# One-hots built 12 blocks at a time in two buffers, in a graph message-passing kernel

## The chip, the cores and the metric

The kernel runs on one core of a Trainium2 chip. The metric is the device time of one execution in microseconds (us), where lower is better. A core has TensorE (PE, with its weight loads as PEld), VectorE (DVE), ScalarE (ACT), GpSimd (POOL) and SyncE (SP), which run their own instruction streams in order and wait for each other on semaphores.

## The reference

A graph with 3125 nodes and 53125 sorted edges passes two layers of messages. Each message is linear, so the sum over the edges of a node needs only the sum of the neighbours' rows, the number of edges and the sum of their attributes.

```python
def _mp_layer(x, src, dst, edge_attr, W, b):
    n = x.shape[0]
    loops = jnp.arange(n, dtype=src.dtype)
    src2 = jnp.concatenate([src, loops])
    dst2 = jnp.concatenate([dst, loops])
    ea2 = jnp.concatenate([edge_attr, jnp.zeros((n, edge_attr.shape[1]), dtype=edge_attr.dtype)], axis=0)
    msg = jnp.concatenate([x[dst2], x[src2], ea2], axis=1) @ W + b
    return jax.nn.relu(jax.ops.segment_sum(msg, dst2, num_segments=n))
...
h = jax.nn.relu(_mp_layer(x, src, dst, edge_attr, W1, b1))
out = jax.nn.log_softmax(_mp_layer(h, src, dst, edge_attr, W2, b2), axis=1)
return _layernorm(x + out, axis=-1)
```

## The kernel before

The 3125 nodes are 25 tiles of 125 nodes. The kernel makes the adjacency matrix in bf16 once, in a tensor `adj`, and then multiplies it with the node rows of layer 1 (x, written as three bf16 parts in `x3`) and of layer 2 (`z3`, three parts too).

**Edges to keys.** The edges fall into 625 blocks (in the code: windows) of at most 128 edges; block w holds the edges into five consecutive target nodes. GpSimd gathers the edges in five groups of 125 blocks (`gather_edges(j)`, `gather_attrs(j)`). VectorE turns each edge into two numbers, seven operations per group (`key_distances`, `key_tiles`, `key_sums`). TensorE turns them around (`turn_keys`) and ScalarE copies them to `keys` (`copy_keys`), one column per block.

**Keys to the matrix.** VectorE makes two one-hot tensors from each column of keys: `ohl` and `ohr`, 125 columns each (`onehots`). TensorE multiplies the two, one matmul per block, into PSUM (`build(k)`: set k is the blocks 8k to 8k+7). ScalarE copies each set from `pset` to `adj` (`evacuate(k)`). There are 79 sets. The one-hots of a set lie in one of three buffers, so `onehots(k)` waits until set k-3 is built: `dve.wait_ge(built, k - 2)`.

**Layer 1.** The matmuls with x3 use the same block numbers: group g of 25 blocks is the target tile g. TensorE's order is written by hand:

```python
for b in range(NSETS):
    if b + LEAD < NSETS:
        build(b + LEAD)
    ...
        layer1(g, h, h + n)
```

LEAD is 4. So one set is built (8 matmuls), then eight matmuls of layer 1 that stand four sets behind, and so on. After each three groups there is an epilogue i, spread over three successive sets b by `turn_block(i)`: `turn_sums`, `hidden`, `messages`. VectorE does its smaller work after the one-hots of particular sets k: the group sums `reduce_sums(g)` at `last_set_block(g) + 6`, `z_rest(i)` and `z_low(i)` of the epilogues, the keys of the next group, the attribute sums and once the bias weights (at k = 10).

**Layer 2** starts when the last set has been used: 625 matmuls (`layer2`), with VectorE's final softmax and normalisation in six batches behind it.

**The start.** SyncE loads the first 12 tiles of x, the weights and the bias rows, and loads the other 13 tiles of x once the first edges have come. ScalarE casts x to its first part (`cast_x`), VectorE subtracts that (`x_rest`), ScalarE casts the middle part, VectorE makes the low part; the first `layer1` waits for all of it. GpSimd splits the bias rows into three bf16 parts (`blink`) after all ten gathers.

Of the kernel before, what the change touches and what calls it, by code (L numbers as in the profile page):

```python
# [68 lines left out]
ROUND = 12582912.0  # L69
MID = N // 2  # L70
# [3 lines left out]
def gnn(nc, x, x_tiles, dst, edges, edge_attr, W1, b1, W2, b2, out, E):  # L74
# [3 lines left out]
    with ExitStack() as ctx:  # L78
        def sb(name, shape, dt):
            return ctx.enter_context(nc.sbuf_tensor(name, shape, dt))  # L80
# [53 lines left out]
        hi_q = tail([Q, J, SLOTS], FP32)  # L134
        lo_f = tail([Q, J, SLOTS], FP32)
        hi_f = tail([Q, J, SLOTS], FP32)
        w_f = tail([Q, J, SLOTS], FP32)
        p_f = tail([Q, J, SLOTS], FP32)
# [23 lines left out]
        ohl = [sb(f"ohl{s}", [128, SET // 2, Q, 2], BF16) for s in range(3)]  # L162
        ohr = [sb(f"ohr{s}", [128, SET // 2, G * WD, 2], BF16) for s in range(3)]
# [124 lines left out]
        xs_ready = sem("xs_ready")  # L288
        bchain = sem("bias_chain")
# [33 lines left out]
        def _(gp):  # L323
# [18 lines left out]
            gp.iota(iota2[:, :, :], [[1, SLOTS], [0, 2]], base=0, channel_multiplier=0,  # L342
# [18 lines left out]
            gather_edges(0)  # L361
            gather_attrs(0)
# [24 lines left out]

            p0, p1, p2 = (bpart[:, k, :] for k in range(3))
            r0, r1 = brest[:, 0, :], brest[:, 1, :]
            done = [1]  # L390

            def blink(ins):
                done[0] += 1
                ins.then_inc(bchain, 1)
                gp.wait_ge(bchain, done[0])

            gp.wait_ge(bchain, 1)
            gp.wait_ge(b_in, 16 * 4)
            blink(gp.tensor_copy(p0, brows))
            blink(gp.tensor_tensor(r0, brows, p0, ALU.subtract))  # L400
            blink(gp.tensor_copy(p1, r0))
            blink(gp.tensor_tensor(r1, r0, p1, ALU.subtract))
            gp.tensor_copy(p2, r1).then_inc(bchain, 1)
# [35 lines left out]
        def _(dve):  # L439
# [51 lines left out]
            def key_distances(j):  # L491

                dve.wait_ge(pairs_in[j], 16)
                dve.wait_ge(loops_ready, 2)
                ins = dve.tensor_scalar(d_f[:, j, :], pairs[:, j, 1::2], thr[:, j:j + 1], None, ALU.subtract)
                dve.tensor_scalar(hi_q[:, j, :], pairs[:, j, 0::2], 1.0 / Q, 0.5 / Q - 0.5, ALU.mult, ALU.add)
                link(ins)

            def key_tiles(j):

                link(dve.scalar_tensor_tensor(out=w_f[:, j, :], in0=d_f[:, j, :], scalar=-float(WD - 1),
                                              in1=d_f[:, j, :], op0=ALU.add, op1=ALU.mult))
                link(dve.tensor_scalar(hi_f[:, j, :], hi_q[:, j, :], ROUND, ROUND, ALU.add, ALU.subtract))

            def key_sums(j):

                dve.tensor_scalar(p_f[:, j, :], w_f[:, j, :], 0.0, 8192.0, ALU.is_gt, ALU.mult)
                link(dve.scalar_tensor_tensor(out=m_f[:, j, :], in0=hi_f[:, j, :], scalar=float(WD),
                                              in1=d_f[:, j, :], op0=ALU.mult, op1=ALU.add))
                dve.scalar_tensor_tensor(out=lo_f[:, j, :], in0=hi_f[:, j, :], scalar=-float(Q), in1=pairs[:, j, 0::2],  # L510
                                         op0=ALU.mult, op1=ALU.add)
                dve.tensor_tensor(key_f[:, j, :], m_f[:, j, :], p_f[:, j, :], ALU.add).then_inc(key_ready, 1)
# [9 lines left out]
            def onehots(k):  # L522

                n = -(-set_size(k) // 2)
                if k >= 3:
                    dve.wait_ge(built, k - 2)
                for oh, key in ((ohl, keyl), (ohr, keyr)):
                    ins = dve.tensor_tensor(  # L528
                        out=oh[k % 3][:, 0:n, :, :],
                        in0=iota2[:, 0:Q, :].unsqueeze(1).broadcast_to([128, n, Q, 2]),  # L530
                        in1=key[:, k * SET:k * SET + 2 * n].rearrange("p (q o k) -> p q o k", o=1, k=2)
                        .broadcast_to([128, n, Q, 2]),
                        op=ALU.is_equal)
                ins.then_inc(oh_ready, 1)

# [28 lines left out]
            key_distances(0)  # L564
            key_tiles(0)
            key_sums(0)
            dve.wait_ge(consts, 8)
            dve.wait_ge(keys_ready, 1)
            for k in range(3):
                onehots(k)  # L570
            dve.wait_ge(xs_ready, 2)
            dve.tensor_tensor(x_rest, x_nat[:, :, :], x3[:, :, 0:C], ALU.subtract).then_inc(xs_rest, 1)
            onehots(3)
            dve.wait_ge(xs_ready, 3)
            dve.tensor_tensor(x3[:, :, 2 * XC:2 * XC + C], x_rest, x3[:, :, XC:XC + C], ALU.subtract).then_inc(xs_ready, 1)
            attr_sums(0, 0, WD)

            for k in range(4, NSETS):
                for j in range(1, J):
                    if k * SET <= j * Q < (k + 1) * SET:  # L580
                        dve.wait_ge(keys_ready, j + 1)
                onehots(k)
# [167 lines left out]
        def _(act):  # L750
# [11 lines left out]

            cast_x(0, 0, XA)

            def copy_keys(bank, j):
                act.wait_ge(keyt_done, j + 1)
                act.activation(keys[:, :, j * Q:(j + 1) * Q], bank.rearrange("p (t w) -> p t w", t=2), ACT.Copy)\  # L767
                   .then_inc(keys_ready, 1)

            copy_keys(acc[0][:, 0:2 * Q], 0)  # L770
            cast_x(1, XA, G)
# [52 lines left out]
            for k in range(3):  # L824
                evacuate(k)
            act.wait_ge(xs_rest, 1)
            act.activation(x3[:, :, XC:XC + C], x_rest, ACT.Copy).then_inc(xs_ready, 1)
            evacuate(3)
# [66 lines left out]
        def _(pe):  # L895
# [245 lines left out]
```

## Time and profile before

| | |
|---|---|
| time, median of 3 runs | 218.02 us (217.85 to 218.08) |
| profiled execution, its own time | 218.17 us |
| profiled execution, its span | 216.4 us |
| PE busy | 181.1 us (84%) |
| DVE busy | 175.5 us (81%) |
| ACT busy | 118.6 us (55%) |
| POOL busy | 43.0 us (20%) |

The span is the part of an execution that the profile's rows cover. Busy time is the sum over an engine's instructions, where overlap counts once. A wait is told as idle time of the waiting instruction's engine, with the instruction that ended it.

### The profile page before, as it was taken

How to read it: one execution, taken by the hardware profiler on the slowest of the kernel's cores; microseconds unless marked ns; L12 is line 12 of the kernel's file. 1: busy time of each engine (PE TensorE's matmuls, PEld its weight loads, DVE VectorE, ACT ScalarE, POOL GpSimd, SP SyncE). 2: the span in 40 equal slices, each digit the busy share in tenths (PEclk: the TensorE clock that was granted, in tenths of full speed). 3: DMA queues.
4: the chain of work that ended last, by engine and by line, in shares of the span. 5: the costliest groups of instructions: out<-in, count | busy, mean ns of one | idle time of the engine just before them, and what ended most of it. 6: DMA issues, size and time to landing. Idle time of an engine off the chain costs nothing.

```text
span 216.4 us, 5159 instructions
## 1 busy us (share of the span) xinstructions
PE 181.1 (84%) x2044; PEld 164.2 (76%) x2044; DVE 175.5 (81%) x510; ACT 118.6 (55%) x225; POOL 43.0 (20%) x61
## 2 busy tenths in 40 slices
PE   0516278799989999999899999999999999999920
PEld 0105178687978998888779979989899999999910
DVE  1879799999899999999998999962025956999881
ACT  2415537569878897887887988976221201011110
POOL 7478873002200395004003000000000000000000
PEclk9999999999999999999999999999999999999995
DMA  1433010000000000000000000000000010101000
GB/s 39 104 101 109 23 13 3 0 3 1 5 2 3 2 3 0 3 0 3 0 3 0 5 0 3 2 3 0 3 0 3 0 39 0 23 17 27 18 18 21
DMA packets 8649, 3.25 MB, mean 15 GB/s; under 512 B 7910, under 2 KB 8175, under 8 KB 8625
## 3 DMA queue, kind: packets, MB, share of 16 engines
q1 hardware_dynamic: 7825, 1.98, 4.4%
q0 software_dynamic: 800, 0.93, 1.8%
q8 instruction: 17, 0.28, 0.5%
q14 instruction: 7, 0.06, 0.1%
HBM read 2.09 MB, written 0.81 MB: 13 GB/s over the span
## 4 chain that ended last, share of the span: by engine, by line
PE 60%; DVE 24%; DMA 7%; ACT 3%; issue 3%; ACTq 0%; DVEq 0%
PE pset L975 17%; PE acc L932 15%; PE pset L918 12%; PE acc L975 8%; DVE ohr L528 7%; DVE ohl L528 6%; DMA x_nat<-in_x_tiles 3%; PE epb L959 3%; DMA adj<-in_edges,adj 2%; DMA adj<-in_dst 2%; PE epb L947 2%; PE epb L967 2%; DVE adj L518 1%; ACT adj L784 1%; PE epb L960 1%
## 5 line engine op out<-in xcount | busy, mean ns | idle before, releaser
L784 ACT ACTIVATE adj<-pset 125x1000 bf16<-125x1000 f32 (+7 forms) x100 | 81.1, 837 | 19.2 <-PE pset L918 15.2
L932 PE MATMUL acc<-x,adj 125*125 125x195 bf16 x625 | 67.1, 250 | 0.0
L918 PE MATMUL pset<-ohr,ohl 128*125 128x125 bf16 x625 | 54.7, 232 | 13.8 <-DVE ohr L528 11.5
L918 PEld LDWEIGHTS pset<-ohr,ohl 128*125 128x125 bf16 x625 | 46.9, 145 | 20.0 <-issue 9.3
L932 PEld LDWEIGHTS acc<-x,adj 125*125 125x125 bf16 x625 | 56.4, 138 | 0.3
L528 DVE TENSOR_TENSOR ohl<-iota,keys 128x1000 bf16<-128x1000 bf16 (+1 forms) x79 | 53.1, 672 | 1.4 <-ACT keys L767 1.3
L528 DVE TENSOR_TENSOR ohr<-iota,keys 128x1000 bf16<-128x1000 bf16 (+1 forms) x79 | 52.9, 669 | 0.0
L975 PE MATMUL pset<-z,adj 125*125 125x192 bf16 x425 | 36.9, 247 | 0.0
L975 PEld LDWEIGHTS pset<-z,adj 125*125 125x125 bf16 x425 | 35.5, 136 | 0.4 <-issue 0.2
L860 ACT ACTIVATE x<-x 125x192 f32<-125x192 f32 (+2 forms) x6 | 2.6, 426 | 31.7 <-DVE x L651 31.7
L377 POOL CAST stats<-se 125x15 bf16<-125x15 f32 x5 | 5.8, 1164 | 66.1 <-DMA se<-se_scratch 66.1
L975 PE MATMUL acc<-z,adj 125*125 125x192 bf16 x200 | 17.6, 247 | 0.0
L975 PEld LDWEIGHTS acc<-z,adj 125*125 125x125 bf16 x200 | 16.8, 136 | 0.1
L542 DVE TENSOR_REDUCE u<-acc 125x65 f32<-125x195 f32 x25 | 8.8, 354 | 6.1 <-PE acc L932 6.0
L550 DVE TENSOR_TENSOR u<-epb,z 125x192 f32<-125x192 f32 (+1 forms) x9 | 3.1, 340 | 11.5 <-ACT z L817 11.5
L358 POOL DMA_INDIRECT adj<-in_edge_attr,adj x5 | 9.2, 1833 | 1.5 <-issue 1.5
L901 PE MATMUL pset<-adj 125*125 125x426 f16 x4 | 2.2, 608 | 7.3 <-DVE adj L459 7.3
L354 POOL DMA_INDIRECT adj<-in_edges,adj x5 | 6.8, 1368 | 4.2 <-DVE adj L476 3.0
L816 ACT ACTIVATE base<-epb 125x192 f32<-125x192 f32 (+1 forms) x9 | 2.9, 319 | 8.7 <-PE epb L969 8.7
L901 PEld LDWEIGHTS pset<-adj 125*125 125x125 f16 x4 | 0.7, 180 | 8.3 <-DVE adj L449 6.1
L641 DVE TENSOR_REDUCE x<-pset 125x64 f32<-125x192 f32 x17 | 5.5, 351 | 1.8 <-PE pset L975 1.7
L799 ACT ACTIVATE u<-x_nat,u 125x64 f32<-125x64 f32 x25 | 6.8, 338 | 0.0
(123 smaller groups left out, 180.0 us busy)
## 6 DMA issues: line engine op xcount, KB each, us to landing
x_nat<-in_x_tiles SPq DMA_DIRECT2D x1, 406.2 KB
x_nat<-in_x_tiles SPq DMA_DIRECT2D x1, 375.0 KB
out<-x SPq DMA_DIRECT2D x2, 187.5 KB
out<-x SPq DMA_DIRECT2D x3, 93.8 KB
adj<-in_dst SPq DMA_DIRECT2D x1, 208.5 KB
out<-x SPq DMA_DIRECT2D x1, 125.0 KB
adj<-in_edges,adj POOLq DMA_INDIRECT x5, 4.4
adj<-in_edge_attr,adj POOLq DMA_INDIRECT x5, 4.5
```

Source lines behind the costliest of these rows:

```text
L354: gp.indirect_dma_start(pairs[:, j, 0:2 * (SLOTS - LOOPS)], None, edges, bass.IndirectOffsetOnAxis(off_idx[:, j:j + 1], 0)).then_inc(pairs ...
L358: gp.indirect_dma_start(attrs[:, j, 0:SLOTS - LOOPS], None, edge_attr, bass.IndirectOffsetOnAxis(off_idx[:, j:j + 1], 0)).then_inc(attrs_i ...
L377: gp.tensor_copy(s0, v.unsqueeze(2).broadcast_to(wide)).then_inc(sech, 1)
L528: ins = dve.tensor_tensor(out=oh[k % 3][:, 0:n, :, :], in0=iota2[:, 0:Q, :].unsqueeze(1).broadcast_to([128, n, Q, 2]), in1=key[:, k * SET: ...
L542: dve.tensor_reduce(u[i % 2][:, m, C:2 * C + 1], acc[g % 2][0:Q, 0:XW].rearrange("p (t c) -> p c t", t=3), AX.X, ALU.add)\
L641: dve.tensor_reduce(f_o[:, g - a, :], bank2(g)[0:Q, :].rearrange("p (t c) -> p c t", t=3), AX.X, ALU.add).then_inc(acc2_read, 1)
L784: ins = act.activation(adj4[0:Q, g, :, i * WD:(i + n) * WD].rearrange("p h (w e) -> p h w e", e=WD), rows[:, w - k * SET:w - k * SET + n, ...
L799: ins = act.activation(u[i % 2][:, m, 0:C], x_nat[:, a + m, :], ACT.Copy, scale=u[i % 2][:, m, 2 * C:2 * C + 1])
L918: ins = pe.matmul(pset[k % 2][0:Q, i // 4, i % 4 * 128:i % 4 * 128 + WD * G], ohl[k % 3][:, i // 2, :, i % 2], ohr[k % 3][:, i // 2, :, i ...
L932: ins = pe.matmul(acc[g % 2][0:Q, 0:XW], adj4[0:Q, g, h, :], x3[:, h, :], start=(h == 0), stop=(h == G - 1))
L959: pe.matmul(epb[:, 0, 0:n], w1c[:, :], flat(i)[:, 0:n], start=True, stop=False)
L975: ins = pe.matmul(bank2(g)[0:Q, :], adj4[0:Q, g, h, :], z3[:, h, :], start=(h == 0), stop=(h == G - 1))
```

## The change

Four edits are made together.

1. The one-hots are no longer made per set of 8 blocks in three buffers. They are made per chunk: the first chunk has 8 blocks, the second 6, then 12 each (14, 26, 38, ...), in two buffers of 12 blocks. Chunk c waits until the set is built that holds the last block of chunk c-2. A set waits for the chunk of its last block. VectorE's smaller work of set k comes after the chunk that holds the set's first block (`beside`).
2. A group's keys take six VectorE operations instead of seven, and two ScalarE copies instead of one.
3. The rest and the low part of x are made in two halves (12 and 13 tiles) at other places of the VectorE and ScalarE streams.
4. GpSimd splits the biases between `gather_edges(0)` and `gather_attrs(0)`.

```diff
+CHUNK = 12
+CHUNKS = ((0, 8), (8, 14)) + tuple((a, min(a + CHUNK, WINDOWS)) for a in range(14, WINDOWS, CHUNK))
+
+
+def chunk_of(w):
+    return next(c for c, (a, b) in enumerate(CHUNKS) if a <= w < b)
...
-        ohl = [sb(f"ohl{s}", [128, SET // 2, Q, 2], BF16) for s in range(3)]
-        ohr = [sb(f"ohr{s}", [128, SET // 2, G * WD, 2], BF16) for s in range(3)]
+        ohl = [sb(f"ohl{s}", [128, CHUNK // 2, Q, 2], BF16) for s in range(2)]
+        ohr = [sb(f"ohr{s}", [128, CHUNK // 2, G * WD, 2], BF16) for s in range(2)]
...
-                ins = dve.tensor_scalar(d_f[:, j, :], pairs[:, j, 1::2], thr[:, j:j + 1], None, ALU.subtract)
-                dve.tensor_scalar(hi_q[:, j, :], pairs[:, j, 0::2], 1.0 / Q, 0.5 / Q - 0.5, ALU.mult, ALU.add)
-                link(ins)
+                dve.tensor_scalar(d_f[:, j, :], pairs[:, j, 1::2], thr[:, j:j + 1], None, ALU.subtract)
+                link(dve.tensor_scalar(q_f[:, j, :], pairs[:, j, 0::2], -float(Q // 2), 1.0 / Q, ALU.add, ALU.mult))
...
-            def onehots(k):
-
-                n = -(-set_size(k) // 2)
-                if k >= 3:
-                    dve.wait_ge(built, k - 2)
+            def onehots(c):
+
+                a, b = CHUNKS[c]
+                n = (b - a + 1) // 2
+                if c >= 2:
+                    dve.wait_ge(built, (CHUNKS[c - 2][1] - 1) // SET + 1)
                 for oh, key in ((ohl, keyl), (ohr, keyr)):
                     ins = dve.tensor_tensor(
-                        out=oh[k % 3][:, 0:n, :, :],
+                        out=oh[c % 2][:, 0:n, :, :],
...
+            key_distances(0)
+            key_tiles(0)
+            key_sums(0)
+            rest_of_x(0, 0, XA)
+            dve.wait_ge(consts, 8)
+            dve.wait_ge(keys_ready, 1)
+            onehots(0)
+            onehots(1)
+            low_of_x(0, 0, XA)
+            onehots(2)
+            rest_of_x(1, XA, G)
+            attr_sums(0, 0, WD)
+            onehots(3)
+            low_of_x(1, XA, G)
+
+            done_sets = 0
+            for c in range(4, len(CHUNKS)):
+                for j in range(1, J):
+                    if CHUNKS[c][0] <= j * Q < CHUNKS[c][1]:
+                        dve.wait_ge(keys_ready, j + 1)
+                onehots(c)
+                sets = range(done_sets, (CHUNKS[c][1] - 1) // SET + 1)
+                done_sets = sets.stop
+                for k in sets:
+                    beside(k)
...
-                pe.wait_ge(oh_ready, k + 1)
+                pe.wait_ge(oh_ready, chunk_of(k * SET + set_size(k) - 1) + 1)
                 for i in range(set_size(k)):
+                    w = k * SET + i
+                    c = chunk_of(w)
+                    q, t = divmod(w - CHUNKS[c][0], 2)
                     ins = pe.matmul(pset[k % 2][0:Q, i // 4, i % 4 * 128:i % 4 * 128 + WD * G],
-                                    ohl[k % 3][:, i // 2, :, i % 2], ohr[k % 3][:, i // 2, :, i % 2], start=True, stop=True)
+                                    ohl[c % 2][:, q, :, t], ohr[c % 2][:, q, :, t], start=True, stop=True)
```

The instruction order of VectorE at the start, from the keys of the first group to the one-hots that the first layer-1 matmuls need (`adj` stands for the scratch tensors that lie in its tail). Before:

```order
L528 TENSOR_TENSOR ohl2<-iota2,keys 128x1000
L528 TENSOR_TENSOR ohr2<-iota2,keys 128x1000
L572 TENSOR_TENSOR adj<-x_nat,x3 125x1600 [waits xs_ready]
L528 TENSOR_TENSOR ohl0<-iota2,keys 128x1000 [waits built]
L528 TENSOR_TENSOR ohr0<-iota2,keys 128x1000
L575 TENSOR_TENSOR x3<-adj,x3 125x25x64 [waits xs_ready]
L518 SCALAR_TENSOR_TENSOR adj<-adj 125x128 [waits attrs_in0]
L518 SCALAR_TENSOR_TENSOR adj<-adj 125x128 x4
L528 TENSOR_TENSOR ohl1<-iota2,keys 128x1000 [waits built]
```

and after the change:

```order
L547 TENSOR_TENSOR adj<-x_nat,x3 125x768 [waits xs_ready]
L536 TENSOR_TENSOR ohl0<-iota2,keys 128x1000 [waits keys_ready,consts]
L536 TENSOR_TENSOR ohr0<-iota2,keys 128x1000
L536 TENSOR_TENSOR ohl1<-iota2,keys 128x750
L536 TENSOR_TENSOR ohr1<-iota2,keys 128x750
L552 TENSOR_TENSOR x3<-adj,x3 125x12x64 [waits xm_ready]
L536 TENSOR_TENSOR ohl0<-iota2,keys 128x1500 [waits built]
L536 TENSOR_TENSOR ohr0<-iota2,keys 128x1500
L547 TENSOR_TENSOR adj<-x_nat,x3 125x832 [waits xs_ready]
```

One subtraction over 25 tiles (`x_rest`) has become one over 12 ahead of the first one-hots and one over 13 behind the third chunk; the low part is split likewise.

VectorE in the long middle stretch, before:

```order
L528 TENSOR_TENSOR ohr1<-iota2,keys 128x1000
L518 SCALAR_TENSOR_TENSOR adj<-adj 125x128 [waits attrs_in2]
L528 TENSOR_TENSOR ohl2<-iota2,keys 128x1000 [waits built]
L528 TENSOR_TENSOR ohr2<-iota2,keys 128x1000
L518 SCALAR_TENSOR_TENSOR adj<-adj 125x128 [waits attrs_in2]
L528 TENSOR_TENSOR ohl0<-iota2,keys 128x1000 [waits built]
```

and after:

```order
L536 TENSOR_TENSOR ohr1<-iota2,keys 128x1500
L561 TENSOR_REDUCE u0<-acc0 125x65 [waits acc_done]
L536 TENSOR_TENSOR ohl0<-iota2,keys 128x1500 [waits built]
L536 TENSOR_TENSOR ohr0<-iota2,keys 128x1500
L580 TENSOR_TENSOR z3<-u1,z3 125x3x64 [waits mid_ready]
L536 TENSOR_TENSOR ohl1<-iota2,keys 128x1500 [waits built]
```

Each pair of one-hot operations still begins with a wait for `built`, but it covers 1500 elements in place of 1000, and the buffers alternate between two.

TensorE, sets 4 to 6 and the layer-1 matmuls between them, before:

```order
L918 MATMUL pset0<-ohr1,ohl1 125x125 [waits oh_ready,evac]
L918 MATMUL pset0<-ohr1,ohl1 125x125 x7
L932 MATMUL acc0<-x3,adj 125x195 [waits keys_ready,xs_ready,evac]
L932 MATMUL acc0<-x3,adj 125x195 x7
L918 MATMUL pset1<-ohr2,ohl2 125x125 [waits oh_ready,evac]
L918 MATMUL pset1<-ohr2,ohl2 125x125 x7
L932 MATMUL acc0<-x3,adj 125x195 x8
L918 MATMUL pset0<-ohr0,ohl0 125x125 [waits oh_ready,evac]
L918 MATMUL pset0<-ohr0,ohl0 125x125 x7
```

and after:

```order
L956 MATMUL pset0<-ohr1,ohl1 125x125 [waits oh_ready,evac]
L956 MATMUL pset0<-ohr1,ohl1 125x125 x5
L956 MATMUL pset0<-ohr0,ohl0 125x125 x2
L970 MATMUL acc0<-x3,adj 125x195 [waits keys_ready,xl_ready,evac]
L970 MATMUL acc0<-x3,adj 125x195 x7
L956 MATMUL pset1<-ohr0,ohl0 125x125 [waits oh_ready,evac]
L956 MATMUL pset1<-ohr0,ohl0 125x125 x7
L970 MATMUL acc0<-x3,adj 125x195 x8
L956 MATMUL pset0<-ohr0,ohl0 125x125 [waits oh_ready,evac]
L956 MATMUL pset0<-ohr0,ohl0 125x125
L956 MATMUL pset0<-ohr1,ohl1 125x125 x6
```

The order of the sets has not moved. Sets 4 and 6 now read from both buffers: 6 blocks from one and 2 from the other, then 2 and 6, while set 5 lies in one buffer.

## Rows read from the trace of the kernel before

**Rows 1.** The page: busy time by engine, and TensorE's granted clock in 40 slices.

```profile
span 216.4 us, 5159 instructions
PE 181.1 (84%) x2044; PEld 164.2 (76%) x2044; DVE 175.5 (81%) x510; ACT 118.6 (55%) x225; POOL 43.0 (20%) x61
...
PEclk9999999999999999999999999999999999999995
```

**Rows 2.** The page: the chain that ended last, shares by line.

```profile
PE pset L975 17%; PE acc L932 15%; PE pset L918 12%; PE acc L975 8%; DVE ohr L528 7%; DVE ohl L528 6%; DMA x_nat<-in_x_tiles 3%; PE epb L959 3%; DMA adj<-in_edges,adj 2%; DMA adj<-in_dst 2%; PE epb L947 2%; PE epb L967 2%; DVE adj L518 1%; ACT adj L784 1%; PE epb L960 1%
```

**Rows 3.** The list of waits: total us, times, longest us.

```profile
PE pset L918 <- DVE ohr L528: 11.5, 11, 4.7
```

**Rows 4.** Timeline of DVE, one-hots; columns are start us, us, instruction.

```profile
39.22 0.66 DVE L528 TENSOR_TENSOR ohl<-iota,keys 128x1000 bf16<-128x1000 bf16 x1
39.81 0.66 DVE L528 TENSOR_TENSOR ohr<-iota,keys 128x1000 bf16<-128x1000 bf16 x1
...
144.19 0.28 DVE L528 TENSOR_TENSOR ohl<-iota,keys 128x250 bf16<-128x250 bf16 x1
```

**Rows 5.** Timeline of PE: a set that waited, and two that did not.

```profile
40.61 0.67 PE L918 MATMUL pset<-ohr,ohl 128*125 128x125 bf16 x8 [0.93 <-DVE ohr L528]
41.12 0.85 PE L932 MATMUL acc<-x,adj 125*125 125x195 bf16 x8
...
132.35 0.64 PE L918 MATMUL pset<-ohr,ohl 128*125 128x125 bf16 x8
...
133.52 0.65 PE L918 MATMUL pset<-ohr,ohl 128*125 128x125 bf16 x8
```

**Rows 6.** Timeline: a group sum on DVE, which waited for PE.

```profile
116.68 0.85 PE L932 MATMUL acc<-x,adj 125*125 125x195 bf16 x8
...
116.96 0.36 DVE L542 TENSOR_REDUCE u<-acc 125x65 f32<-125x195 f32 x1 [0.62 <-PE acc L932]
```

**Rows 7.** Timeline of PE: sets around one epilogue, and set 76.

```profile
94.28 0.67 PE L918 MATMUL pset<-ohr,ohl 128*125 128x125 bf16 x8
...
96.21 0.70 PE L918 MATMUL pset<-ohr,ohl 128*125 128x125 bf16 x8
...
98.44 0.70 PE L918 MATMUL pset<-ohr,ohl 128*125 128x125 bf16 x8
...
100.73 0.70 PE L918 MATMUL pset<-ohr,ohl 128*125 128x125 bf16 x8
...
144.85 0.70 PE L918 MATMUL pset<-ohr,ohl 128*125 128x125 bf16 x8
```

**Rows 8.** Timeline of DVE: the biases' first operation, an epilogue's rest, the next one-hots.

```profile
38.10 0.30 DVE L587 TENSOR_SCALAR adj<-adj,bmask 12x192 f32<-12x192 bf16 x1
...
56.49 0.36 DVE L550 TENSOR_TENSOR u<-epb,z 125x192 f32<-125x192 f32 x1
...
57.34 0.67 DVE L528 TENSOR_TENSOR ohl<-iota,keys 128x1000 bf16<-128x1000 bf16 x1
```

**Rows 9.** Timeline of the start: DVE, then PE (sets 4 and 6).

```profile
12.58 0.29 DVE L495 TENSOR_SCALAR adj<-adj,thr 125x128 f32<-125x128 int32 x1
...
15.77 0.68 DVE L528 TENSOR_TENSOR ohl<-iota,keys 128x1000 bf16<-128x1000 bf16 x1 [1.32 <-ACT keys L767]
...
23.89 1.83 DVE L575 TENSOR_TENSOR x<-adj,x 125x1600 bf16<-125x1600 f32 x1 [1.57 <-ACT x L827]
...
28.03 0.99 DVE L528 TENSOR_TENSOR ohl<-iota,keys 128x1000 bf16<-128x1000 bf16 x1
...
28.25 1.08 PE L918 MATMUL pset<-ohr,ohl 128*125 128x125 bf16 x8 [4.69 <-DVE ohr L528]
...
31.92 0.64 PE L918 MATMUL pset<-ohr,ohl 128*125 128x125 bf16 x8
```

**Rows 10.** Timeline of POOL: first and last of five operations that split the biases.

```profile
26.81 0.76 POOL L399 CAST adj<-adj 12x192 bf16<-12x192 f32 x1
...
30.20 0.67 POOL L403 CAST adj<-adj 12x192 bf16<-12x192 f32 x1
```

More of the change, by code:

```diff
@@ L69 @@
 ROUND = 12582912.0
+LIFT = 64.0
+CODE = 128.0
 MID = N // 2
@@ L288, in gnn @@
         xs_ready = sem("xs_ready")
+        xm_ready = sem("xm_ready")
+        xl_ready = sem("xl_ready")
         bchain = sem("bias_chain")
@@ L361, in _, with blink @@
             gather_edges(0)
+            p0, p1, p2 = (bpart[:, k, :] for k in range(3))
+            r0, r1 = brest[:, 0, :], brest[:, 1, :]
+            done = [1]
+            def blink(ins):
+                done[0] += 1
+                ins.then_inc(bchain, 1)
+                gp.wait_ge(bchain, done[0])
+            gp.wait_ge(bchain, 1)
+            gp.wait_ge(b_in, 16 * 4)
+            blink(gp.tensor_copy(p0, brows))
+            blink(gp.tensor_tensor(r0, brows, p0, ALU.subtract))
+            blink(gp.tensor_copy(p1, r0))
+            blink(gp.tensor_tensor(r1, r0, p1, ALU.subtract))
+            gp.tensor_copy(p2, r1).then_inc(bchain, 1)
             gather_attrs(0)
@@ L385, in split_sums @@
                 gp.tensor_copy(s2, r[:, :, 1:2].broadcast_to(wide)).then_inc(se_parts, 1)
[L388 to L403, printed above, removed]
             for j in range(J):
@@ L562, in z_low, with beside @@
                    .then_inc(z3_ready, 1)
[L564 to L582, printed above, removed]
+            def beside(k):
                 if k == 10:
@@ L761, in cast_x, with cast_middle_x @@
                 act.activation(x3[:, a:b, 0:C], x_nat[:, a:b, :], ACT.Copy).then_inc(xs_ready, 1)
+            def cast_middle_x(i, a, b):
+                act.wait_ge(xs_rest, i + 1)
+                act.activation(x3[:, a:b, XC:XC + C], x_rest[:, a:b, :], ACT.Copy).then_inc(xm_ready, 1)
             cast_x(0, 0, XA)
@@ L766, in copy_keys @@
                 act.wait_ge(keyt_done, j + 1)
-                act.activation(keys[:, :, j * Q:(j + 1) * Q], bank.rearrange("p (t w) -> p t w", t=2), ACT.Copy)\
-                   .then_inc(keys_ready, 1)
+                act.activation(keyl[:, j * Q:(j + 1) * Q], bank[:, 0:Q], ACT.Copy, scale=float(Q),
+                               bias=float(Q // 2) + Q * LIFT + CODE)
+                act.activation(keyr[:, j * Q:(j + 1) * Q], bank[:, Q:2 * Q], ACT.Copy, scale=float(WD),
+                               bias=CODE - WD * LIFT).then_inc(keys_ready, 1)
             copy_keys(acc[0][:, 0:2 * Q], 0)
-            cast_x(1, XA, G)
+            cast_middle_x(0, 0, XA)
             def evacuate(k):
@@ L822, in cast_middle @@
                 act.activation(z3[:, a:b, C:2 * C], u[i % 2][:, 0:b - a, 0:C], ACT.Copy).then_inc(mid_ready, 1)
-            for k in range(3):
+            evacuate(0)
+            cast_x(1, XA, G)
+            evacuate(1)
+            cast_middle_x(1, XA, G)
+            for k in range(2, LEAD):
                 evacuate(k)
-            act.wait_ge(xs_rest, 1)
-            act.activation(x3[:, :, XC:XC + C], x_rest, ACT.Copy).then_inc(xs_ready, 1)
-            evacuate(3)
             for b in range(NSETS):
```

32 lines of the change are left out of this document (17 added, 15 removed).

## The prediction

> **What bounds the kernel now.** I read the page first: PE is busy 84% of the span and DVE 81% [rows 1], so either could bound it. The chain of work that ended last tells more: most of it is matmuls, but 13% is the two one-hot operations of L528 [rows 2]. The list of waits says the same from the other side: PE's sets waited 11.5 us for one-hots in 11 places [rows 3]. Then I read the timelines of both engines from the first set to the last. Where PE does not wait, a set with its eight layer-1 matmuls takes 1.17 us (132.35 to 133.52) [rows 5]; a pair of one-hot operations takes 2 x 0.59 = 1.18 us (start to start 39.22 to 39.81) [rows 4], plus DVE's smaller work. So the two run neck and neck, and three buffers keep them loosely coupled. From set 4 (28.25) [rows 9] to set 76 (144.85) [rows 7] the kernel takes 116.60 us for 72 sets, 1.62 us a set. Behind that comes layer 2, which the change does not touch.
>
> **Part 1: the chunks.** What they promise is fewer DVE instructions: 53 pairs instead of 79. An operation over 1000 elements took 0.66 us, one over 250 took 0.28 [rows 4]: 0.38 us for 750 elements, 0.51 for 1000. The fixed part of the 0.59 us step is thus 0.08 us, and 52 operations fewer save about 4 us of DVE time. An operation over 1500 elements steps 0.59 + 0.25 = 0.85 us and lasts about 0.93.
>
> What they cost is in the wait. The chunks end at blocks 14, 26, 38, 50, ..., and 14 + 12m is never a multiple of 8. Chunk c may begin when the set is built that holds the last block of chunk c-2. That set always holds blocks of chunk c-1 too (the order of PE shows it: 6 blocks from one buffer, 2 from the other), and it can't be built before chunk c-1 is whole. So chunk c can't begin before chunk c-1 has been made, and has been used by a whole set. Two buffers are there, but DVE and PE take turns. One turn, from the start of such a straddling set:
>
> - the set's last matmul ends 0.67 us after its first began [rows 5], and DVE starts about 0.02 later;
> - DVE makes the pair: 0.85 + 0.93 = 1.78 us;
> - PE starts 0.14 us after DVE's end: 39.81 + 0.66 = 40.47 to 40.61 [rows 4, 5].
>
> The sum is 2.61, with rounding 2.62 us for 12 blocks, or 1.75 us a set, where PE needs 1.17. From set 4 (first of chunk 4) to set 76 (first of chunk 52) there are 48 turns: 48 x 2.62 = 125.8 us, as a floor. Three things make single turns longer. I went through all 48, with VectorE's and TensorE's work of each turn from the order:
>
> - *PE's epilogues.* Turns hold one set and two sets in alternation. With an epilogue's parts the distance between sets is 1.93, 2.23 and 2.29 us instead of 1.17 [rows 7]. In a one-set turn this fits into 2.62. In a two-set turn it does not: three turns hold hidden and messages (4.51 us each), two hold sums and hidden (4.18 each, the sums' part lying in the first set) and one the messages alone (3.45). Together 3 x 1.89 + 2 x 1.56 + 0.83 = 9.6 us more.
> - *Group sums.* `reduce_sums(g)` stands behind the chunk that holds the first block of set k. For g = 0 to 7 that set is the second one after the straddling set, and DVE must wait in its place for layer-1 matmuls that PE runs only after the straddling set. The group ends after n matmuls of a piece: n = 2 ended 0.28 us after the piece's start [rows 6], and a matmul more is 0.09. The next chunk begins 0.20 + 0.09 n late. For g = 1 to 6 (n = 2 to 7), with what stands behind the sum in two of them, this is about 4.1 us.
> - *DVE's other work.* Slack for it is 0.69 + 0.14 + 0.07 = 0.9 us a turn. z_rest takes 0.85 (56.49 to 57.34), the bias weights 1.12 (38.10 to 39.22) [rows 4, 8], a group's last key operations some 0.7. Alone they fit or nearly; in eight turns they come together or with the first and last of the eight sums. I count 3.6 us.
>
> So set 4 to set 76 takes 125.8 + 9.6 + 4.1 + 3.6 = 143.1 us at PE's warm pace. One more term: set 4 took 1.08 us where later ones take 0.64 to 0.67 [rows 5, 9], and set 6 started 3.67 us after set 4 rather than 2.34. PE itself bounds that turn, 3.67 instead of 2.62: 1.05 us. Sum 144.2 us against 116.6: **27.6 us more**.
>
> **Part 2: keys.** One dependent operation of about 0.25 us goes from each group. Only the first group's lies on the path: DVE works on it from 12.58, and the one-hots start at 15.77 [rows 9]. ACT's two copies instead of one take about 0.14 us more (a second fixed part, estimated). The later groups' saving is inside the 3.6 above.
>
> **Part 3: x in halves.** Before, DVE stood 1.57 us waiting for ACT's middle part (ahead of 23.89), and 1.32 us for the keys (ahead of 15.77) [rows 9]. The first half's rest, about 0.84 us (1.83 for 25 tiles [rows 9], so 12/25 of it), now fills the second of these, and the 1.57 us are filled by chunks. Against it, set 4 needs 50 blocks instead of 40 (10 blocks x 2 x 0.064 = 1.3 us), and chunk 4 waits some 0.3 us for set 3.
>
> **Part 4: biases.** GpSimd's five operations last 4.06 us (26.81 to 30.87) [rows 10]. In that time a one-hot operation took 0.99 us in place of 0.66 [rows 4, 9]: DVE slows beside them. They now lie beside the first keys. I take 0.4 us of slowing for the key operations, which eats what part 2 gains; bounds are 0 and the whole 4.1 us. By the Trainium skill, page "SBUF — State Buffer", section "SBUF: two separate sides", GpSimd and VectorE hold their shared port pair as an exclusive lock for a whole instruction; by that rule the six key operations could each wait for a GpSimd operation of 0.7 to 0.8 us, so some 2 us or more instead of 0.4. The row on the one-hots shows only 0.33 for one, so I keep 0.4. The gathers behind move about 4 to 6 us later; the attribute sums of group 0 stand after 21 us now, and nothing else needs them soon.
>
> Parts 2 to 4 on the start of set 4: -1.57 - 0.84 + 1.3 + 0.3 + 0.14 - 0.25 + 0.4 = -0.5, I take **-0.6 us** (the slowed one-hot at 28.03 goes too).
>
> **The sum.** 218.17 (the profiled execution; 0.15 above the median) + 27.6 - 0.6 = 245.2; at the end some of VectorE's waits for the last epilogues have been served already, -0.3; on the scale of the median 244.7 us.
>
> **The rivals.**
>
> *A. The turns do not arise* (faster). If DVE can run a chunk ahead after all, PE and DVE overlap as before, and the 4 us of DVE time count where DVE was on the chain, about half, with 0.6 from the start: 218.0 - 2 - 0.6 = 215.4 us. It decides at the mean turn: 116.6/48 = 2.43 us; below that the change wins. For it: both engines need less than that alone (1.76 and 1.70 us per 12 blocks). Against: the waits of the order are not a matter of durations. Chance 6%.
>
> *B. PE's pace falls* (much slower). PE is busy only 1.76 of 2.62 us in a turn. The profile gives the granted clock as 9 throughout [rows 1], yet sets took 1.08 us at 28.25 and 0.64 at 31.92 [rows 9], a half-speed (1.2 GHz) and a full-speed (2.4 GHz) pace. PE had been mostly idle before the slow ones. If it fell back, a turn is 0.41 us longer by the set's end, and a two-set turn about 4.3 us: per pair of turns 7.4 instead of 5.24, so up to 52 us over 24 pairs; half the time, 271 us. Against: a pause of 0.93 us ahead of 40.61 left that set at 0.67 [rows 5]; mine would be up to 1.5. By the Trainium skill, page "TensorE: Matmul & The Clock Gate", section "HAM oscillation — how this bites in real kernels", it is long waits between bursts of matmuls that bring the low clock back; short pauses would then change nothing. Chance 6%.
>
> *C. Turns, but cheaper or dearer pieces.* The same mechanism with a turn off by 0.1 us moves the sum by 4.8; the epilogues' 9.6 us could partly be hidden (minus 5) and the keys' slowing be 2 us more. This is the width of my own case: 237 to 252.
>
> **How the numbers follow.** My case with its width has 88%, rivals A and B 6% each. The range 237 to 254 leaves out both tails. Changes under 0.2% (0.4 us) can't be told from none here. Faster 0.06, same 0.02, slower 0.92.
>
> **What would show it.** After: L536 about 0.93 us for 1500 elements; starts of the pairs about 2.62 us apart in quiet stretches, each right behind the end of a set; waits of PE on one-hots and of DVE on `pset` matmuls in nearly every turn, tens of us in all; the first layer-1 piece half a microsecond earlier; layer 2 as long as before, but beginning some 27 us later. I would be wrong if DVE's pairs follow each other without waits, or if PE's sets of 8 matmuls last over 1 us.

## The result and the profile after

| | before | after |
|---|---|---|
| time, median | 217.94 us (217.72 to 218.08, 4 runs) | 251.34 us (247.00 to 251.66, 4 runs) |
| profiled execution, its own time | 218.17 us | 247.00 us |
| profiled execution, its span | 216.4 us | 245.2 us |

Its executions differ by the granted clock of TensorE: one with a mean of 0.987 took 247.00 us, one more (not in the table) with 0.977 took 250.30, three with 0.967 to 0.970 took 251.1 to 251.7. The changed kernel takes 1.141 times as long, interval 1.128 to 1.154, by its two quicker executions; by the median of 251.34 it would be 1.153. The profiled execution is the 247.00, the quickest of all.

The page of the kernel after: busy time by engine, and the granted clock.

```profile
span 245.2 us, 5103 instructions
PE 183.3 (75%) x2044; PEld 164.3 (67%) x2044; DVE 173.0 (71%) x450; ACT 119.9 (49%) x231; POOL 29.8 (12%) x61
...
PEclk9999999999999999999999999999999999999995
...
PE pset L956 15%; PE pset L1013 15%; DVE ohr L536 13%; DVE ohl L536 12%; PE acc L970 10%; PE acc L1013 7%; PE epb L997 2%; DMA adj<-in_dst 2%; DVE adj L484 1%; PE epb L1005 1%; DVE base L571 1%; DVE u L561 1%; DVE adj L525 1%; PE epb L985 1%; PE epb L998 1%
```

DVE saved only 2.5 us of busy time, and both engines' shares fell from over 80% [rows 1] to 75% and 71%: neither is the bound by itself any more. In the chain of work that ended last, the one-hots rose from 13% [rows 2] to 25%. A chain that changes sides between two engines, neither of them busy, is what taking turns looks like on a page.

The list of waits of the kernel after (total us, times, longest us) shows the turns from both sides.

```profile
PE pset L956 <- DVE ohr L536: 38.5, 35, 2.4
...
DVE ohl L536 <- PE pset L956: 28.7, 32, 2.7
```

Before, the first stood at 11.5 us [rows 3], and the second was not in the list of waits at all. Now 32 of DVE's pairs wait for PE and 35 of PE's sets wait for DVE. The timelines of the kernel after show single turns, first on PE:

```profile
27.97 1.09 PE L956 MATMUL pset<-ohr,ohl 128*125 128x125 bf16 x8 [1.97 <-DVE ohr L536]
28.85 1.51 PE L970 MATMUL acc<-x,adj 125*125 125x195 bf16 x8
30.16 0.91 PE L956 MATMUL pset<-ohr,ohl 128*125 128x125 bf16 x8
30.90 0.85 PE L970 MATMUL acc<-x,adj 125*125 125x195 bf16 x8
31.60 0.65 PE L956 MATMUL pset<-ohr,ohl 128*125 128x125 bf16 x8
...
85.31 0.67 PE L956 MATMUL pset<-ohr,ohl 128*125 128x125 bf16 x8
...
87.96 0.67 PE L956 MATMUL pset<-ohr,ohl 128*125 128x125 bf16 x8 [1.28 <-DVE ohr L536]
...
95.45 0.70 PE L956 MATMUL pset<-ohr,ohl 128*125 128x125 bf16 x8
...
97.73 0.70 PE L956 MATMUL pset<-ohr,ohl 128*125 128x125 bf16 x8
...
173.71 0.67 PE L956 MATMUL pset<-ohr,ohl 128*125 128x125 bf16 x8 [0.32 <-DVE ohr L536]
```

and on DVE:

```profile
86.02 0.94 DVE L536 TENSOR_TENSOR ohl<-iota,keys 128x1500 bf16<-128x1500 bf16 x1 [0.58 <-PE pset L956]
86.88 0.93 DVE L536 TENSOR_TENSOR ohr<-iota,keys 128x1500 bf16<-128x1500 bf16 x1
...
88.66 0.94 DVE L536 TENSOR_TENSOR ohl<-iota,keys 128x1500 bf16<-128x1500 bf16 x1 [0.58 <-PE pset L956]
```

The set at 85.31 ends 0.67 later, at 85.98; DVE starts the pair at 86.02 and ends it at 87.81; PE's next set starts at 87.96, 2.65 us after the first. The second operation of the pair stands for its full 0.93 us, since none follows at once. Set 4 starts at 27.97 and set 76 at 173.71: 145.74 us, where it was 116.60.

### The profile page after: what moved, and what is told of

It is laid out like the page before. It is cut to its first block, busy times and chain, and to the rows that moved or that the text cites. A ratio compares the mean times of both kernels' runs of the same rounds, so it can differ in the third digit from the quotient of the medians.

```text
span 245.2 us, 5103 instructions
## 1 busy us (share of the span) xinstructions
PE 183.3 (75%) x2044; PEld 164.3 (67%) x2044; DVE 173.0 (71%) x450; ACT 119.9 (49%) x231; POOL 29.8 (12%) x61
## 3 DMA queue, kind: packets, MB, share of 16 engines
q1 hardware_dynamic: 7825, 1.98, 3.8%
## 4 chain that ended last, share of the span: by engine, by line
PE 52%; DVE 37%; issue 5%; DMA 2%; ACT 1%; DVEq 0%
PE pset L956 15%; PE pset L1013 15%; DVE ohr L536 13%; DVE ohl L536 12%; PE acc L970 10%; PE acc L1013 7%; PE epb L997 2%; DMA adj<-in_dst 2%; DVE adj L484 1%; PE epb L1005 1%; DVE base L571 1%; DVE u L561 1%; DVE adj L525 1%; PE epb L985 1%; PE epb L998 1%
## 5 line engine op out<-in xcount | busy, mean ns | idle before, releaser
L956 PE MATMUL pset<-ohr,ohl 128*125 128x125 bf16 x625 | 54.4, 232 | 39.9 <-DVE ohr L536 38.5
L956 PEld LDWEIGHTS pset<-ohr,ohl 128*125 128x125 bf16 x625 | 46.4, 145 | 48.6 <-ACT adj L818 31.6
L536 DVE TENSOR_TENSOR ohl<-iota,keys 128x1500 bf16<-128x1500 bf16 (+2 forms) x53 | 49.0, 925 | 29.2 <-PE pset L956 28.7
L536 DVE TENSOR_TENSOR ohr<-iota,keys 128x1500 bf16<-128x1500 bf16 (+2 forms) x53 | 48.8, 920 | 0.0
L405 POOL CAST stats<-se 125x15 bf16<-125x15 f32 x5 | 2.0, 399 | 94.7 <-DMA se<-se_scratch 94.7
L368 POOL DMA_INDIRECT adj<-in_edge_attr,adj x5 | 7.4, 1476 | 1.4 <-issue 1.4
L1005 PE MATMUL epb<-w2c,turn 128*125 128x128 f32 x48 | 6.7, 277 | 0.0
```

The lines of the kernel that those rows point to most:

```text
L368: gp.indirect_dma_start(attrs[:, j, 0:SLOTS - LOOPS], None, edge_attr, bass.IndirectOffsetOnAxis(off_idx[:, j:j + 1], 0)).then_inc(attrs_i ...
L536: ins = dve.tensor_tensor(out=oh[c % 2][:, 0:n, :, :], in0=iota2[:, 0:Q, :].unsqueeze(1).broadcast_to([128, n, Q, 2]), in1=key[:, a:a + 2 ...
L1005: pe.matmul(z_cols(b - a)[:, m, :], flat(i)[:, m * Q:(m + 1) * Q], w2c[:, :], start=True, stop=True)
```

## Experiments

Except where it is said, each kernel is the changed one with the edit shown. Kernels that were timed together share their runs of the kernel before: 217.99 us for the first four, 217.37 for the next four and 218.02 for the last four. Kernels of different groups are therefore compared by their ratio to it.

### Half of the chunk ends on set ends

```diff
-CHUNKS = ((0, 8), (8, 14)) + tuple((a, min(a + CHUNK, WINDOWS)) for a in range(14, WINDOWS, CHUNK))
+CHUNKS = ((0, 8), (8, 16)) + tuple((a, min(a + CHUNK, WINDOWS)) for a in range(16, WINDOWS, CHUNK))
```

Still 12 blocks in two buffers, but every second chunk ends where a set ends.

> The changed kernel with the second chunk 8 blocks long instead of 6, so that chunks end at 16, 28, 40, 52, ...: every second end is a multiple of 8. Nothing else changes: 12 blocks, two buffers. Theory 'turns' (a chunk can't begin before a set is built that itself needs the chunk before): only every second chunk is locked now. Three sets then take 0.69 + 1.70 + 1.78 + 0.14 = 4.31 us as a floor instead of 2 x 2.64 = 5.28, below what PE needs with its epilogues on average (4.5), so most of the loss goes: 225 to 233 us, and VectorE's waits for built sets fall to less than half. Rival 'two buffers are too few' or 'chunks of 12 are too coarse': neither has changed, so 246 us or more.

Measured: 233.44 us (230.93 to 233.80), ratio 1.068 (1.061 to 1.075). One shifted number takes about half of the loss back. PE's waits for one-hots fell from 38.5 to 21.5 us and DVE's for sets from 28.7 to 20.7, where less than half had been expected. The median lies just above the expected range; the execution with clock 0.987 took 230.93, those with 0.961 some 233.8. The clock fell here too, after a long pause. PE's timeline of this kernel:

```profile
96.25 0.85 PE L957 MATMUL pset<-ohr,ohl 128*125 128x125 bf16 x8 [2.59 <-DVE ohr L537]
96.89 1.51 PE L971 MATMUL acc<-x,adj 125*125 125x195 bf16 x8
```

### Chunks as large as sets, in two buffers

```diff
-CHUNK = 12
-CHUNKS = ((0, 8), (8, 14)) + tuple((a, min(a + CHUNK, WINDOWS)) for a in range(14, WINDOWS, CHUNK))
+CHUNK = 8
+CHUNKS = tuple((a, min(a + CHUNK, WINDOWS)) for a in range(0, WINDOWS, CHUNK))
```

> The changed kernel with chunks of 8 blocks, which are the sets themselves, in two buffers (16 blocks in all instead of 24). Theory 'turns': no chunk end lies inside a set, so chunk c waits for set c-2, while set c-1 lies ready for PE: a set can follow every 2.08/2 = 1.04 us, less than PE's 1.17; 217 to 226 us with a shorter lead for VectorE's smaller work, about 221. Rival 'two buffers are too few': the lead is a third shorter than in the changed kernel, so at least 246 us, more likely above 250.

Measured: 222.56 us (222.41 to 223.21), ratio 1.022 (1.020 to 1.024). The same number of buffers with smaller chunks wins back 29 of the 33 us. So two buffers by themselves are not what costs most. This run alone does not tell the chunk ends from the chunk size; the one above does, where the size stayed at 12 and only the ends moved.

### Chunks as large as sets, in three buffers

The edit above, with three buffers (`range(3)`, `c % 3`, and the wait on chunk c-3). This is the kernel before with parts 2 to 4 alone.

> The changed kernel with chunks of 8 blocks in three buffers: the one-hots as before the change, with the new keys, the split x and the early biases kept. 'Turns' says that all of the loss was in the chunks: set 4 starts near 26.2 us (five pairs, 5.9, the three x operations behind the first pair, 2.7, attribute sums, 1.06, from 16.31) instead of 28.25, and the time is 216 to 218 us. Rival 'the other three parts cost too': above 219 us.

Measured: 213.93 us (213.64 to 214.01), ratio 0.981 (0.979 to 0.983), faster than before by more than expected. PE's timeline of this kernel, sets 4 and 76:

```profile
26.21 1.09 PE L957 MATMUL pset<-ohr,ohl 128*125 128x125 bf16 x8 [1.03 <-DVE ohr L537]
...
140.63 0.70 PE L957 MATMUL pset<-ohr,ohl 128*125 128x125 bf16 x8
```

Set 4 comes 2.04 us earlier than before, as expected. But the 72 sets behind it take 114.42 us instead of 116.60, 2.2 us less, which I had not counted on.

This kernel is also the right base for the loss, since parts 2 to 4 are in it. With the same parts, two buffers of 8 cost 8.6 us (222.56) and the chunks of 12 another 28.8 (251.34): 37.4 us in all, of which the other parts' gain hides 4. So the third buffer is worth something too. Three buffers of 12 blocks were not run.

### Unequal buffers of 16 and 8 blocks

```diff
+BUF = (16, 8)
+CHUNKS = ((0, 8), (8, 16)) + tuple((a + 16 * h, min(a + 16 + 8 * h, WINDOWS)) for a in range(16, WINDOWS, 24) for h in (0, 1) if a + 16 * h < WINDOWS)
```

The same memory and as few chunks as in the change, but all ends lie on set ends.

> The changed kernel with chunks of 16 and 8 blocks by turns in two buffers of 16 and 8 blocks: as many blocks of buffer (24) and as many one-hot operations as in the changed kernel (53 pairs and one or two), but every end is a multiple of 8. 'Turns': three sets have a floor of 0.69 + 2.27 + 0.14 + 1.17 = 4.25 us, below PE's mean of 4.5 with epilogues; 215 to 224 us, about 219. Rival 'two buffers are too few' or 'large chunks are too coarse': 245 us or more.

Measured: 226.99 us (226.41 to 227.61), ratio 1.040 (1.037 to 1.043). The expectation was too optimistic by 8 us and its range was missed, though 24 us better than the change. A quiet stretch of three sets (from 74.99 to 79.32 in its timeline) takes 4.33 us, where 4.25 were expected, so the quiet pace was right. From set 4 to set 76 this profile takes 126.00 us, where the kernel before took 116.60, so the whole loss lies there. A part is a stretch at the lower clock behind a pause of 1.85 us (ahead of 113.88); the rest presumably lies in turns with other work, which was not taken apart.

### The change again, in more executions

> The changed kernel once more, as it is. Its five times so far were 247.0, 250.3, 251.1, 251.6 and 251.7 us, with a mean granted clock of 0.987, 0.977 and three times 0.967: the longer, the lower. Theory 'clock': in a turn PE pauses for up to 2.4 us, and in some executions the chip grants it half the pace for a few us behind a pause; then the times keep lying between 247 and 252, in the order of the granted clock. Rival 'something else': times without relation to the clock.

Measured: 250.47 us (247.02 to 251.21), ratio 1.148 (1.143 to 1.153). The profiled execution took 251.21. Its page gives the clock as

```profile
PEclk9999999979999999999979999979999999999995
```

and PE's timeline of this execution shows one of the three places:

```profile
124.57 0.67 PE L956 MATMUL pset<-ohr,ohl 128*125 128x125 bf16 x8 [0.94 <-DVE ohr L536]
...
127.48 1.08 PE L956 MATMUL pset<-ohr,ohl 128*125 128x125 bf16 x8 [1.54 <-DVE ohr L536]
128.35 1.51 PE L970 MATMUL acc<-x,adj 125*125 125x195 bf16 x8
...
130.08 0.83 PE L956 MATMUL pset<-ohr,ohl 128*125 128x125 bf16 x8
130.75 0.85 PE L970 MATMUL acc<-x,adj 125*125 125x195 bf16 x8
```

Sets of 1.08 us and pieces of 1.51 are the pace of the cold start (27.97 above), the 1.2 GHz level, and the granted clock reads 0.50 in such a stretch (128.00 to 130.00). The three stretches stand behind pauses of 1.29, 1.54 and 1.28 us. The span is 249.4 against 245.2, 1.4 us for each. The quick execution paused at the same places for as long, and its set behind the 1.54 us is quick:

```profile
125.89 0.67 PE L956 MATMUL pset<-ohr,ohl 128*125 128x125 bf16 x8 [1.54 <-DVE ohr L536]
```

From 32 us on, each of the two profiles has 16 pauses of 1.2 us or more ahead of a set; three of them are followed by a fall here and none there. So such a pause allows the fall but does not decide it.

### Unused matmuls in the pauses

```diff
+                    if i == b * SET and h > 0 and b % 3 == 2 and b + LEAD < NSETS:
+                        for r in range(12):
+                            pe.matmul(acc[g % 2][0:Q, 256:256 + 128], adj4[0:Q, g, h, :], x3[:, h, 0:128], start=False, stop=False)
```

In 24 places, all but one of them one-set turns, PE gets twelve matmuls more, whose results nobody reads. This asks whether the clock, and not more waiting, makes the median 4 us longer than the quick execution.

> The changed kernel with 12 more matmuls of 128 columns (into columns of the acc bank that nobody reads) ahead of the layer-1 piece in two of three one-set turns, where PE pauses 1.3 to 1.5 us. They add about 0.7 us of PE work per such turn, inside the pause. Theory 'clock': with the pauses halved the granted clock stays near 0.985 and all times lie near 247 us, 3 to 4 below the changed kernel's median. Rival 'something else': the median stays at 251 us or more.

Measured: 252.24 us (251.86 to 252.69), ratio 1.161 (1.159 to 1.162). The mean clock was 0.979 to 0.986 in all runs, and the profile has no stretch at half pace behind the cold start, yet the kernel was not faster. The profile's span is 5.1 us longer than that of the quick execution (250.3 against 245.2). Of this, 2.0 us lie between set 4 and set 76. In turns with an epilogue's part PE had no room: the turn whose set starts at 73.78 in the kernel after lasts 2.65 us, and here (74.16 to 77.06) 2.90. Another part lies at the very end. VectorE's last operation, in the kernel after and then here:

```profile
240.38 0.36 DVE L705 TENSOR_TENSOR x<-x 125x192 f32<-125x192 f32 x1
...
242.68 0.36 DVE L706 TENSOR_TENSOR x<-x 125x192 f32<-125x192 f32 x1
```

From its end to the end of the span there are 4.5 us in the kernel after, 4.4 to 4.5 in every other profile, and 7.3 here. These 2.8 us have no part in the turns, and what causes them is open. Up to VectorE's last operation this execution is 1.9 us shorter than the change run again (243.04 against 244.94). The experiment mixed several effects and does not decide the question, so it was made again without the turns that hold an epilogue's part.

### Unused matmuls only in turns without an epilogue

The edit above, with the condition that no part of an epilogue lies in set b (216 matmuls instead of 288).

> The changed kernel (12 blocks, two buffers) with the 12 extra matmuls only in one-set turns that hold no epilogue part, so that each fits into the pause (0.5 + 0.7 + 0.7 = 1.9 of 2.64 us). Theory 'clock': fewer or no stretches at half pace, the granted clock 0.98 or more, the time 247 to 249 us with little spread, below the changed kernel's usual 250.5. Rival 'the half-paced stretches cost nothing by themselves': 250 us or more although the granted clock is 0.98 or more.

Measured: 248.16 us (247.25 to 248.82), ratio 1.139 (1.136 to 1.142), clock 0.986 to 0.989 in every run. Though PE has more to do, this is 0.8% less than the 1.148 of the change itself, and the intervals do not overlap. Single stretches of the two profiles (columns: window, its length, busy us of PE, PEld, DVE, ACT, POOL, granted clock, DMA share, GB/s), first the change run again:

```profile
40.00:60.00 20.00, 15.48 (x165) 13.84 (x166) 12.84 (x26) 11.52 (x20) 2.34 (x5) 0.91 0.03 1
...
120.00:140.00 20.00, 15.98 (x164) 14.09 (x164) 14.42 (x36) 12.37 (x24) 2.11 (x5) 0.91 0.02 1
```

and then this one:

```profile
40.00:60.00 20.00, 17.24 (x208) 15.20 (x207) 14.13 (x26) 12.82 (x22) 1.58 (x5) 1.00 0.03 2
...
120.00:140.00 20.00, 17.18 (x206) 15.30 (x205) 15.84 (x38) 13.49 (x25) 1.38 (x5) 1.00 0.02 1
```

With the pauses filled, the granted clock stays at 1.00, and the wasted work costs less than the falls did. The quick execution of the kernel after reads 1.00 in these two windows too, with PE busy for 15.75 and 15.77 us. So what the filling changes is how often the clock falls: nine of the eleven executions of the change had a mean clock of 0.977 or less, and none of the six here.

### The chunks alone

The kernel before with part 1 only: its keys, its x in one piece, its biases behind the gathers.

> The kernel before with part 1 alone: chunks of 8, 6, 12, 12, ... blocks in two buffers; old keys, x in one piece, biases behind the gathers. 'Turns': the whole loss is here, and the start is slower than the changed kernel's (VectorE again stands for x's middle part, and set 4 now needs 50 blocks): set 4 near 29.5 us instead of 27.97, so 1 to 3 us above the changed kernel, 249 to 254 us. Rival 'the other parts cost too': below 247 us.

Measured: 253.89 us (253.24 to 255.47), ratio 1.169 (1.166 to 1.172), at the upper end of what was expected and 3.4 us above the change in the same group, where 1 to 3 were. Set 4 starts at 30.05. The chunks alone cost more than the whole change does. They save DVE almost nothing: it is busy for 175.1 us, where it was 175.5 before. Here too the clock falls (mean 0.961 to 0.967 in all four runs), once behind a pause of only 1.07 us (ahead of 111.65), with one of 1.89 us ahead of the set before it.

The biases lie behind the gathers in this kernel, and one of the five GpSimd operations meets VectorE's long x operation:

```profile
24.20 1.93 DVE L613 TENSOR_TENSOR x<-adj,x 125x1600 bf16<-125x1600 f32 x1 [1.16 <-ACT x L844]
...
24.54 1.98 POOL L408 TENSOR_TENSOR adj<-adj 12x192 f32<-12x192 f32 x1
```

The same GpSimd operation took 0.83 us in the kernel before. Here it lasts 1.98 and ends 0.39 behind VectorE's.

### Parts 2 to 4 taken one by one

All on the kernel with chunks of 8 in three buffers. First, the biases go back behind the gathers.

> The 8x3 kernel (sets in three buffers, other parts kept) with the bias splits back behind the gathers. The five GpSimd operations then lie beside the one-hots again, which cost 1.1 us of VectorE time before the change, while beside the keys they made the first one-hots start at 16.3 instead of 15.7 us (0.5 us late). Theory 'VectorE bounds the first 20 us, so its time counts wherever it is lost': 0.3 to 0.7 us slower than 8x3, 214.2 to 214.7. Rival 'the start of the keys counts most': 0.3 to 0.6 us faster, 213.3 to 213.6.

Measured: 213.56 us (213.38 to 213.88), ratio 0.983 (0.982 to 0.984). The intervals of this ratio and of 0.981 overlap: no difference that can be told, and neither theory is confirmed. DVE's timelines show why. With the biases early (the three-buffer kernel) the keys run beside them:

```profile
13.30 0.56 DVE L512 TENSOR_SCALAR adj<-adj 125x128 f32<-125x128 f32 x1
13.90 0.43 DVE L516 SCALAR_TENSOR_TENSOR adj<-adj 125x128 f32<-125x128 f32 x1
...
16.27 0.68 DVE L537 TENSOR_TENSOR ohl<-iota,keys 128x1000 bf16<-128x1000 bf16 x1 [0.51 <-ACT keys L802]
```

With the biases late, the keys are quick and the first one-hots start 0.82 us earlier, but later ones run beside the same five GpSimd operations:

```profile
12.93 0.29 DVE L512 TENSOR_SCALAR adj<-adj 125x128 f32<-125x128 f32 x1
13.25 0.29 DVE L516 SCALAR_TENSOR_TENSOR adj<-adj 125x128 f32<-125x128 f32 x1
...
15.45 0.68 DVE L537 TENSOR_TENSOR ohl<-iota,keys 128x1000 bf16<-128x1000 bf16 x1 [0.51 <-ACT keys L802]
...
26.48 0.99 DVE L537 TENSOR_TENSOR ohl<-iota,keys 128x1000 bf16<-128x1000 bf16 x1
```

The slowing is paid in either place: set 76 starts at 140.63 and at 140.56.

The three-buffer kernel again, beside the two below:

> The 8x3 kernel once more, on the same chip as the next ones, so that they can be compared with it. 213.9 us as before, 0.981 of the kernel before.

Measured: 213.92 us (213.68 to 213.96), ratio 0.981 (0.979 to 0.983).

Then x in one piece (`rest_of_x(0, 0, G)` and `low_of_x(0, 0, G)` around `onehots(3)`, as before):

> 8x3 with x's rest, middle and low part made in one piece again. Theory 'the 4 us of 8x3 come mostly from the split of x, which fills two waits of VectorE': set 4 starts 1.5 to 2 us later (near 28 us instead of 26.2) and the time is 1.2 to 2 us longer, 215.1 to 215.9. Rival 'the keys brought them': less than 0.5 us longer.

Measured: 215.46 us (215.37 to 215.67), ratio 0.988 (0.986 to 0.990). The halves are worth 1.5 us, all of it at the start: set 4 comes at 27.91 instead of 26.17. The size is as expected, but 1.5 is not most of the 4.

Then the keys as before (seven operations, one copy by ScalarE):

> 8x3 with the seven old key operations and the one copy by ACT. Theory 'split of x': four later groups cost about 0.3 us of VectorE time each, the first group next to nothing beside the bias splits: 0.4 to 1.4 us longer than 8x3, 214.3 to 215.3. Rival 'the keys brought them': 2 us longer or more.

Measured: 215.51 us (215.01 to 215.89), ratio 0.988 (0.986 to 0.990). The six operations with the two copies are worth 1.6 us, a little above the expected 0.4 to 1.4, but hardly at the start: set 4 comes at 26.36, only 0.19 later. Set 76 comes at 142.18 instead of 140.59, 1.59 later. The four later groups' keys make the difference.

## Why the prediction was right, and where it was off

Predicted were 244.7 us in a range of 237 to 254; measured were 251.34, in the range but 6.6 us above the value. The prediction's own scale gives 244.9 for the profiled execution, which took 247.00. Point by point:

- **The turns.** Shown. Half of the ends aligned took half of the loss away, all of them with smaller chunks 29 of 33 us. Rival A, that DVE runs ahead after all, is out. A quiet turn was to take 2.62 us and takes 2.64 to 2.65. In the 30 turns that no term below covers, 0.02 us each makes 0.6 us of the miss: even an error as small as the rounding counts when it is multiplied by so many turns.
- **PE's epilogues.** Six two-set turns were to take 4.51 (three), 4.18 (two) and 3.45 us. They took 4.49, 4.49, 4.50, 4.11, 4.10 and 3.60. Above the 2.62 that is 9.57 us, predicted 9.6. Some of this agreement is luck: the last was put 0.15 too short and the others together 0.20 too long. (The rows' distances add to 4.52, 4.16 and 3.46.) One of the three is above: 95.45 to 97.73 is the part from its second set on.
- **Group sums and DVE's other work.** Predicted 4.1 and 3.6. The six two-set turns from 34.29 to 67.36 whose sum must wait are 3.7 us longer than 2.62 each, and the five later two-set turns with DVE work in them 4.0. Beyond 0.02 each, the 24 one-set turns add 1.1, most of it (0.7) in the three that begin at 37.28, 61.07 and 122.98. If these three are taken with the five, there are eight turns, as many as the prediction counted, and they cost 4.7 us instead of 3.6: this is the term that was mis-sized most between set 4 and set 76.
- **The cold first turn.** Predicted 1.05, measured 1.01 (27.97 to 31.60, against 2.62).
- **The sum, set 4 to set 76.** 144.2 predicted, 145.74 measured.
- **The start.** Predicted 0.6 us earlier, measured 0.28 (28.25 to 27.97). The term that was most clearly mis-sized is the slowing beside GpSimd's bias splits: I took 0.4 us. In the three-buffer kernel it is twice that. With the biases late, the x operation behind the keys starts at 13.99, with them early at 14.82: 0.83 us, of which 0.23 is a delay of the keys' start by slowed operations ahead, which I had not looked at. By the Trainium skill, page "SBUF — State Buffer", section "SBUF: two separate sides", the port pair is locked for a whole instruction; from this the prediction estimated 2 us or more for the six operations. The trace does not show this: together they lost 0.60 us, one operation went from 0.29 to 0.56, another from 0.29 to 0.43. In the kernel of the chunks alone the trace agrees with the lock in the other direction, where GpSimd is the one that waits (24.54, 1.98 us). The terms of the start do not simply add. In the kernel with three buffers x in halves brings set 4 forward by 1.74 us, the keys by 0.19, and the early biases put it back by 0.83; that is 1.10 earlier, where the three together gave 2.04. How the 0.3 us of the miss divide is therefore open.
- **The end.** Predicted 0.3 us less behind set 76; measured 71.5 us as against 71.55 before, so nothing to speak of. With 1.54 and 0.32 this closes the account of the profiled execution: 244.9 + 1.5 + 0.3 + 0.2 = 246.9.
- **DVE's time.** Part 1 was to save about 4 us of DVE time. The chunks alone saved 0.4 of its busy time. What the rows suggest: the 0.08 us per operation is saved only where another operation follows at once (step 0.86, length 0.93). In a turn DVE stands still after each pair, so the end of the pair is no longer hidden. The term stood only in rival A, and the sum does not miss it.
- **Rival B.** I set "PE's pace falls" apart as an all-or-nothing case of 6%, up to 271 us. It holds in small, inside my own case: one profiled execution has three stretches at half pace, worth some 4 us, and nine of eleven executions have the lower mean clock that goes with them. That is the larger part of the miss in the median, and the step that failed is the sentence that a pause of 0.93 us left its set at 0.67 and so speaks against it. In the turns the pauses came again and again and were up to 1.5 us, and at 1.3 to 1.5 the fall does sometimes happen. The filled turns show that it is the pauses: PE had more work and the time fell by 0.8%. I also read the page "TensorE: Matmul & The Clock Gate" of the Trainium skill too narrowly. Its section "A second HAM failure mode: psum-queue depth-cycling" tells of another kernel where frequent small idle times between groups of matmuls make the clock go back and forth. With that the runs here agree. Why one execution has three such stretches and another none is open.
- **Where the expected gain is.** Parts 2 to 4 do gain, 1.9% when the three buffers stay: 1.5 us by x in halves, 1.6 by the keys, nothing that can be told by the biases, the remaining microsecond not assigned. For the keys I counted only the first group, since later groups' operations seemed to fit into DVE's slack. Whether they do in turns was not measured by itself; in the kernel with three buffers, where DVE waits for PE's sets only once and for 0.3 us, the four later groups carry 1.4 of the 1.6.

The best version is the one with chunks of 8 in three buffers, 0.981 times the kernel before; where the biases stand makes no difference that can be told.

## What to carry to other kernels

Before a producer's chunk is made larger than its consumer's group, write down for one period which buffers each group reads and which group each chunk waits for: if every group that frees a buffer also needs the chunk in the other, the two engines take turns, and a turn takes the time of that group plus that of the chunk, not the larger of the two. It is then not enough that a second buffer is there: here moving the ends of the chunks, at the same size and in the same two buffers, took back half of the loss. Read such a loss off two waits that point at each other in the list while both engines' shares fall. When a change puts regular pauses into TensorE's work, price a few stretches at half pace too, and not only the all-or-nothing case.

## What was unexpected of the hardware

Pauses of 1.28 to 1.54 us in a stretch where PE was busy for three quarters of the time were followed, in some executions and not in others, by about 3 us at the 1.2 GHz level, costing 1.4 us each. With twelve short matmuls in each of 18 places (PE busy 17.2 of 20 us instead of about 15.8), which left one of the 16 pauses of 1.2 us or more, the granted clock read 1.00 in the middle of the profiled execution, and all six runs had the high mean of 0.986 to 0.989. And GpSimd operations on only 12 partitions slowed VectorE's operations beside them, from 0.29 to 0.56 us and from 0.67 to 0.99, by less than the length of the GpSimd operation beside them (0.52 and 0.83 us, which the profile gives only roughly).
